# Fused attention and gated-recurrence kernel: VectorE's loop instructions read one SBUF tensor at most, two small products move to GpSimd

## The reference

```
c   = cross_attention(x, cond)                    # 16 heads of 8, one key per head: softmax over 16
q,k,v = heads(c @ Wq), heads(c @ Wk), heads(c @ Wv)   # 16 heads h, 8 dims d
q = softmax(q over d);  k = elu(k) + 1
ctx = cumsum over h of k[d] * v[e];   ctx /= cumsum over h of k[d] + eps
x = x + (sum over d of q[d] * ctx[d, e]) @ Wo + bo
for each of the 128 tokens:                       # a gated recurrence, h0 = cond
    m, o = split(sigmoid([x_t, h] @ w_W + w_b))
    h = o * h + (1 - o) * tanh(x_t @ wx_W + wx_b + m * (h @ wh_W + wh_b))
x = x + experts(hs)                               # 8 experts, relu then square, the top 2 by router logits
```

## Time and profile before

| | |
|---|---|
| median of 3 runs | 627.83 us (627.83 to 629.28) |
| span of the profiled execution, first to last instruction | 625.2 us |
| median less that span (the profiled execution has no other time of its own) | 2.6 us |
| busy: TensorE, VectorE, ScalarE, GpSimd | 480.3, 514.4, 291.4, 208.7 us |
| mean granted TensorE clock | 0.806 of full |

### The profile page before, as it was taken

How to read it: one execution, slowest core, us unless ns; L and a number is a source line. 1 busy time by engine, 2 the same in 40 slices (tenths; PEclk the granted TensorE clock), 3 DMA queues, 4 the chain that set the end, 5 groups by cost and what they waited for, 6 DMA issues and landing times.

```text
span 625.2 us, 10470 instructions
## 1 busy us (share of the span) xinstructions
PE 480.3 (77%) x2559; PEld 362.0 (58%) x2559; DVE 514.4 (82%) x1403; ACT 291.4 (47%) x1084; POOL 208.7 (33%) x192
## 2 busy tenths in 40 slices
PE   6998467877777778877777777778877777777897
PEld 4876145556556556665655556556655655555575
DVE  4777799888988888888888988888888888988852
ACT  4554222444544455444444544455444444544465
POOL 5544433333333332222333333332222333333100
PEclk9999555677888888777777788888777777788899
DMA  5210000000000000000000000000000000000000
GB/s 158 71 35 1 0 0 2 0 5 5 6 4 3 5 4 4 4 4 4 4 4 4 4 2 2 4 4 4 4 4 4 4 4 4 4 3 3 8 6 14
DMA packets 12648, 6.44 MB, mean 10 GB/s; under 512 B 801, under 2 KB 12626, under 8 KB 12626
## 3 DMA queue, kind: packets, MB, share of 16 engines
q1 hardware_dynamic: 12626, 6.19, 3.5%
HBM read 4.09 MB, written 2.10 MB: 10 GB/s over the span
## 4 chain that ended last, share of the span: by engine, by line
PE 43%; DVE 38%; issue 12%; ACT 2%; SPq 2%; DVEq 1%; DMA 1%
PE bank L380 36%; DVE kvs L978 9%; DVE wo L1051 7%; DVE wo L1058 7%; DVE h L1066 6%; PE bank L555 4%; ACT to L768 2%; DVE gw L1023 1%; PE bank L510 1%; DVE mem L1044 1%; SPq L243 1%; DVE kv L941 1%; DMA xin<-in_x_dram 1%; PE bank L434 1%; DVE qn L970 1%
## 5 line engine op out<-in xcount | busy, mean ns | idle before, releaser
L363 POOL TENSOR_TENSOR qc<-kvs,qn 128x512 f32<-128x512 f32 x64 | 97.1, 1518 | 348.0 <-DVE qn L970 325.6
L380 PE MATMUL bank<-h,gwh 128*128 128x32 f32 x512 | 108.4, 297 | 119.1 <-DVE h L1066 118.7
L380 PEld LDWEIGHTS bank<-h,gwh 128*128 128x128 f32 x512 | 93.1, 226 | 154.2 <-DVE h L1066 152.7
L380 PE MATMUL bank<-w,h 128*128 128x512 f32 x128 | 92.2, 812 | 0.0
L766 ACT ACTIVATE th<-bank 128x32 f32<-128x32 f32 x128 | 25.5, 199 | 140.0 <-PE bank L380 139.8
L739 ACT ACTIVATE hid<-bank,gw 128x128 f32<-128x128 f32 x256 | 75.8, 365 | 30.5 <-PE bank L380 30.3
L978 DVE TENSOR_TENSOR_SCAN kvs<-scan_mask,kv 128x256 f32<-128x256 f32 x128 | 86.3, 697 | 0.0
L351 POOL TENSOR_TENSOR kv<-kv,qkv 128x512 f32<-128x512 f32 x64 | 79.4, 1260 | 10.6 <-DVE kv L941 10.6
L1066 DVE TENSOR_TENSOR_SCAN h<-tm,wo 128x64 f32<-128x64 f32 x128 | 60.6, 474 | 15.7 <-ACT tm L774 14.2
L1044 DVE TENSOR_TENSOR_SCAN mem<-th,bank 128x64 f32<-128x64 f32 x128 | 34.0, 266 | 45.2 <-PE bank L380 44.9
L380 PEld LDWEIGHTS bank<-w,hsq 128*128 128x128 f32 x512 | 65.2, 194 | 7.4 <-issue 0.5
(11 more groups left out here) (137 smaller groups left out, 820.0 us busy)
## 6 DMA issues: line engine op xcount, KB each, us to landing
xin<-in_x_dram SPq DMA_DIRECT2D x8, 256.0 KB, 2.8
out_dram<-res SPq DMA_DIRECT2D x32, 64.0 KB
w<-in_L_ffn_w_all_dram SPq DMA_DIRECT2D x2, 512.0 KB
gwx<-in_L_cond_w_W_dram SPq DMA_DIRECT2D x1, 128.0 KB
gwh<-in_L_cond_w_W_dram SPq DMA_DIRECT2D x1, 128.0 KB
mbias<-gpart SPq DMA_DIRECT2D x6, 0.2 KB, 1.7
cwk<-in_L_cond_Wk_dram SPq DMA_DIRECT2D x1, 64.0 KB
cwv<-in_L_cond_Wv_dram SPq DMA_DIRECT2D x1, 64.0 KB
```

Of the source, the lines that this page charges most:

```text
L363: pool.tensor_tensor(qc[:, a:b, :, :], kvs[:, a * D:b * D, :].rearrange("p (d e) h -> p d e h", d=D // 2), qn[:, p, a:b, :].unsqueeze(2).b ...
L380: return pe.matmul(dst, w, rhs, start=start, stop=True, skip_group_check=True)
```

## The change

Every VectorE instruction of the main loop gets at most one of its tensors from SBUF. Bank 1 (`DV`) no longer holds a gate but VectorE's small operands: the scan mask (256 columns), `den`, `wo`, `qmax`, `qsum` and the router's `chosen` logits. Both gates stand in bank 0 (`Z`): their bias comes in by a product with ones for both, and one tanh takes both halves after TensorE's second gate product, so the memory's product comes third, not second. `keys` and `queries` become plain two-tensor instructions on GpSimd (the relu on the keys is now a second eviction on ScalarE). The router replaces the logits that are not chosen instead of taking the chosen ones out, so that `two_largest`, `taken` and a copy fall away. `exp_qk` stands one step earlier in ScalarE's queue. VectorE's queue is in a new order: each step's four instructions stand together as `update`, and `finish` comes before the third update, `taken_inverse` directly behind it.

```diff
--- before.py
+++ after.py
@@ -136,23 +131,25 @@
...
-        th = sb("th", [P, B, 2])
-        to = sb("to", [P, B])
+        gt = sb("gt", [P, 2, B, 2])
...
-        wo = sb("wo", [P, B, 2])
...
-        dl, gex = sb("dl", [P, 2, NE]), sb("gex", [P, 2, NE])
...
+        dl = sb("dl", [P, NE])
...
+        scan_mask = DV[:, 0:D * D * H // 4]
+        den = DV[:, 256:384].rearrange("p (d h) -> p d h", h=H)
+        wo = DV[:, 384:448].rearrange("p (b i) -> p b i", i=2)
+        qmax, qsum, chosen = DV[:, 448:464], DV[:, 464:480], DV[:, 480:488]
...
@@ -342,6 +335,18 @@
             split(pool.tensor_tensor(gres[:, 1, :], gres[:, 0, :], gpart[:, 1, :], ALU.subtract))
             pool.tensor_copy(gpart[:, 2, :], gres[:, 1, :]).then_inc(gsplit, 1)
+            def keys(t, p):
+                pool.wait_ge(ex_done, t + 1)
+                at_least(pool, k_sum, t)
+                pool.tensor_tensor(kv[:, D * D:, :], qkv[:, p, 1, :, :], ex[:, p, 1, :, :], ALU.add)\
+                    .then_inc(k_ready, 1)
+            def queries(t, p):
+                pool.wait_ge(d_rec, 2 * t + 2)
+                pool.tensor_tensor(qn[:, p, :, :], ex[:, p, 0, :, :], rden[:, :, :], ALU.mult).then_inc(qn_done, 1)
             def outer(t, p, half):
                 a, b = half * D // 2, (half + 1) * D // 2
@@ -366,7 +371,11 @@
             def iteration(t, p, has):
                 if has(2):
+                    queries(t + 2, p)
                     weigh(t + 2, p, 0)
+                if has(3):
+                    keys(t + 3, 1 - p)
+                if has(2):
                     weigh(t + 2, p, 1)
                 if has(3):
                     outer(t + 3, 1 - p, 0)
@@ -518,11 +527,11 @@
...
-                at_least(pe, th_done, STEPS * t)
-                mm(ZH[:, 0:TOK], hbias[:, :], ones[:, :])
-                mm(ZH[:, 0:TOK], gwx[:, 0:P], xs, start=False)
-                at_least(pe, to_done, STEPS * t)
-                mm(ZO[:, 0:TOK], gwx[:, P:2 * P], xs)
+                at_least(pe, ga_done, STEPS * t)
+                mm(Z[:, 0:TOK], zbias[:, 0:P], ones[:, :])
+                mm(Z[:, TOK:2 * TOK], zbias[:, P:2 * P], ones[:, :], start=False)
+                mm(Z[:, 0:TOK], gwx[:, 0:P], xs, start=False)
+                mm(Z[:, TOK:2 * TOK], gwx[:, P:2 * P], xs, start=False)
...
@@ -570,10 +579,10 @@
...
-                mm(ZH[:, col:col + B], gwh[:, 0:P], h, start=False).then_inc(zh_ps, 1)
+                mm(Z[:, col:col + B], gwh[:, 0:P], h, start=False)
+                mm(Z[:, TOK + col:TOK + col + B], gwh[:, P:2 * P], h, start=False).then_inc(z_ps, 1)
                 mm(MEM[:, 2 * s * B:2 * (s + 1) * B], whw[:, :], h.unsqueeze(2).broadcast_to([P, B, 2]),
...
-                mm(ZO[:, col:col + B], gwh[:, P:2 * P], h, start=False).then_inc(zo_ps, 1)
...
@@ -707,7 +715,9 @@
...
-                act.activation(qkv[:, p, :, :, :].rearrange("p w d h -> p (w d h)"), QKV[:, P:], ACT.Copy)\
+                act.activation(qkv[:, p, 1, :, :].rearrange("p d h -> p (d h)"), QKV[:, 2 * P:3 * P], ACT.Relu)
+                act.activation(qkv[:, p, 0:3:2, :, :].rearrange("p w d h -> p w (d h)"),
+                               QKV[:, P:].rearrange("p (w n) -> p w n", w=3)[:, 0:3:2, :], ACT.Copy)\
...
@@ -752,21 +762,18 @@
...
-            def gate_exp(t):
+            def gate_exp(t, p):
...
-                at_least(act, gw_done, t)
-                act.activation(gex[:, :, :], dl[:, :, :], ACT.Exp, scale=0.5).then_inc(g_exp, 1)
+                act.activation(gw[:, p, :], dl[:, :], ACT.Exp, scale=0.5).then_inc(gw_done, 1)
...
-                act.wait_ge(zh_ps, n + 1)
-                act.activation(th[:, :, 1], ZH[:, col:col + B], ACT.Tanh, scale=0.5).then_inc(th_done, 1)
-                act.wait_ge(zo_ps, n + 1)
-                act.activation(to[:, :], ZO[:, col:col + B], ACT.Tanh, bias=gcol[:, 0:1], scale=0.5)\
-                    .then_inc(to_done, 1)
+                act.wait_ge(z_ps, n + 1)
+                act.activation(gt[:, :, :, 1], Z[:, 0:2 * TOK].rearrange("p (g n) -> p g n", g=2)[:, :, col:col + B],
+                               ACT.Tanh, scale=0.5).then_inc(ga_done, 1)
...
@@ -796,6 +803,8 @@
...
                     memory_tanh(t, 0)
+                if has(3):
+                    exp_qk(t + 3, q)
...
@@ -805,11 +814,9 @@
                 if has(0):
...
-                    gate_exp(t - 1)
+                    gate_exp(t - 1, q)
                 if has(0):
                     memory_tanh(t, 1)
-                if has(3):
-                    exp_qk(t + 3, q)
...
                 if has(0):
@@ -932,42 +943,31 @@
...
-                                  qmax[:, :].unsqueeze(1).broadcast_to([P, D, H]), ALU.subtract).then_inc(ex_ready, 1)
-            def keys(t, p):
+                                  qmax.unsqueeze(1).broadcast_to([P, D, H]), ALU.subtract).then_inc(ex_ready, 1)
+            def query_sum(t, p):
...
-                at_least(dve, kv_done, 2 * t)
-                dve.scalar_tensor_tensor(out=kv[:, D * D:, :], in0=qkv[:, p, 1, :, :], scalar=0.0,
-                                         in1=ex[:, p, 1, :, :], op0=ALU.max, op1=ALU.add).then_inc(k_ready, 1)
-            def query_sum(t, p):
-                dve.tensor_reduce(qsum[:, :], ex[:, p, 0, :, :].rearrange("p d h -> p h d"), AX.X, ALU.add)\
+                dve.tensor_reduce(qsum, ex[:, p, 0, :, :].rearrange("p d h -> p h d"), AX.X, ALU.add)\
...
-                dve.tensor_tensor_scan(flat(kvs[:, D * D:, :]), flat(scan_mask[:, D * D:, :]), flat(kv[:, D * D:, :]),
+                dve.tensor_tensor_scan(flat(kvs[:, D * D:, :]), scan_mask[:, 0:D * H], flat(kv[:, D * D:, :]),
...
-                dve.scalar_tensor_tensor(out=den[:, :, :], in0=kvs[:, D * D:, :], scalar=EPS,
-                                         in1=qsum[:, :].unsqueeze(1).broadcast_to([P, D, H]), op0=ALU.add,
+                dve.scalar_tensor_tensor(out=den, in0=kvs[:, D * D:, :], scalar=EPS,
+                                         in1=qsum.unsqueeze(1).broadcast_to([P, D, H]), op0=ALU.add,
...
+                at_least(dve, qn_done, t)
...
-            def queries(t, p):
-                dve.wait_ge(d_rec, 2 * t + 2)
-                at_least(dve, qc_done, 2 * (t - 1))
-                dve.tensor_tensor(qn[:, p, :, :], ex[:, p, 0, :, :], rden[:, :, :], ALU.mult).then_inc(qn_done, 1)
...
@@ -1039,16 +1031,14 @@
...
-                dve.wait_ge(th_done, n + 1)
+                dve.wait_ge(ga_done, n + 1)
...
-                dve.tensor_tensor_scan(flat(mem[:, :, :]), flat(th[:, :, :]), MEM[:, 2 * s * B:2 * (s + 1) * B],
+                dve.tensor_tensor_scan(flat(mem[:, :, :]), flat(gt[:, 0, :, :]), MEM[:, 2 * s * B:2 * (s + 1) * B],
...
-                n = STEPS * t + s
-                dve.wait_ge(to_done, n + 1)
-                dve.tensor_scalar(wo[:, :, 0], to[:, :], -0.5, 0.5, ALU.mult, ALU.add).then_inc(w_done, 1)
+                dve.tensor_scalar(wo[:, :, 0], gt[:, 1, :, 1], -0.5, 0.5, ALU.mult, ALU.add).then_inc(w_done, 1)
...
@@ -1063,89 +1053,61 @@
                 n = STEPS * t + s
                 dve.wait_ge(tm_done, n + 1)
                 dve.wait_ge(oh_done, n + 1)
-                dve.tensor_tensor_scan(flat(h2[:, p, s, :, :]), flat(tm[:, :, :]), flat(wo[:, :, :]), 0.0, ALU.mult,
+                dve.tensor_tensor_scan(flat(h2[:, p, s, :, :]), flat(tm[:, :, :]), flat(wo), 0.0, ALU.mult,
                                        ALU.add).then_inc(h_done, 1)
+            def update(t, p, s):
+                memory(t, p, s)
+                renewed(t, s)
+                kept(t, p, s)
+                new_h(t, p, s)
             def iteration(t, p, has):
                 q = 1 - p
-                if has(0):
-                    memory(t, p, 0)
-                    renewed(t, 0)
-                if has(-1):
-                    route(t - 1)
-                if has(0):
-                    kept(t, p, 0)
+                if has(2):
+                    inverses(t + 2, 1)
+                if has(1):
+                    add_dims(t + 1, 1)
                 if has(3):
                     head_max(t + 3, q)
-                if has(0):
-                    new_h(t, p, 0)
+                    less_max(t + 3, q)
+                if has(0):
+                    update(t, p, 0)
                 if has(-1):
-                    two_largest(t - 1)
+                    largest_logits(t - 1)
+                    drop_others(t - 1)
                 if has(2):
                     sum_heads(t + 2, 0)
                 if has(-1):
-                    dve.wait_ge(l_lead, t)
-                    dve.wait_ge(l_copy, t)
+                    less_top(t - 1)
                 if has(2):
                     sum_heads(t + 2, 1)
-                elif has(-1):
-                    dve.tensor_copy(gw2[:, 0:1], lead[:, 0:1])
-                if has(-1):
-                    take_out(t - 1)
-                    less_top(t - 1)
-                if has(0):
```

(49 more changed lines are left out.)

89 lines of the change are left out of this document (38 added, 51 removed).

## The result

The changed kernel takes 603.9 us (median of 4 runs, 598.22 to 607.91), beside 627.83 us before (626.4 to 629.28, 4 runs): a ratio of 0.959, 95% interval 0.954 to 0.964. That is faster, by 24 us, but not by the 71 us of the forecast of 557; it lies at the upper end of the range.

A forecast was written before the change was run, and what follows sets the result against it. VectorE instructions held while GpSimd reads SBUF were taken to bound the kernel. Waits of 14.04 plus 0.3 (PSUM) and 0.4 (clock) made 14.7 us per iteration, saving 63 us, plus 7.5 elsewhere: 557 us, range 531 to 604.

The forecast's parts named there:

- the term of the clock: Main loop: TensorE's clock drops in about a quarter of the iterations, 1.5 us each time, taken as 0.4 us per iteration.
- the clock falls in every iteration: Rival, main loop: TensorE's clock drops every iteration, costing 1.5 us each, 15.8 us per iteration, about 587 us; chance 22%.
- m0-m1: Main loop, from the start of an iteration's first memory scan to its second: 2.69 us, limited by VectorE's work.
- m1-m2: Main loop, second to third memory scan: 1.04 us, then 2.84 through TensorE's products and `finish`, an added wait.
- Holds: Main loop: all four VectorE instructions held while GpSimd reads SBUF are freed, 3.9 us per iteration.
- `renewed` is held all the same: Rival, main loop: `renewed` stays held despite writing to PSUM, 16.6 us per iteration, 609 us; chance 8%.
- The loop of waits: Main loop: distances between memory scans sum to 14.04 us per iteration, with waits added ahead of `finish` and `taken_inverse`.
- PSUM operands: Main loop: some 22 VectorE instructions newly read or write PSUM, taken as 0.3 us per iteration.
- GpSimd: Main loop: `queries` and `keys` move to GpSimd at 0.54 us each, hidden with 6.6 us busy of 14.
- Elsewhere: Outside the steady iterations: prologue 5.5 us off, half of iterations 0 and 1's holds off, last three 2 on; 7.5 off.
- a mean clock that stays at 0.8: Sign in the profile after, on TensorE: it would show the prediction wrong; a clock above 0.85 was expected.
- The rival in which TensorE is the bound at the lower clock throughout: Main loop: TensorE without idle at 19.3 us per iteration, slower, about 685 us; chance 5%.

The follow-up runs named there:

- e1: The changed kernel with three unread products on TensorE, two ahead of the fourth step and one ahead of `x_rows`: 540.54 us.
- e9: The changed kernel with only two unread products on TensorE, ahead of the fourth step: 551.55 us.
- e7: The changed kernel with `taken_inverse` alone put back behind the fourth memory scan, `finish` staying ahead of the third step: 522.76 us.
- e8: As e2, but with the 64-column operand `wo` alone moved back from PSUM to SBUF: 595.39 us.
- e2: The changed kernel with `finish` and `taken_inverse` both put back behind the fourth memory scan: 467.23 us.

## Why the forecast was too low

**The step that failed is the term of the clock**: "I take 0.4, a drop in about a quarter of the iterations". It was 2.7 us per iteration from t = 5 to 27 (17.07 against 14.29 and 0.1 for the loop's turn), and 64.6 us over all 27 iterations (450.35 here, 385.74 in e1), where 0.4 times 27 is 11. The 54 us between are more than the whole miss of 47. Two things in the term were wrong.

- How often. The argument against a fall was that no idle time is as long as the 3.85 us that came before the fall in the old kernel. That took the one idle stretch seen at a fall for the least that brings one, and it misread the stretch: its row has a clock of 0.81, so the fall came inside it, about 2.4 us after its start (2 x 0.19 x 3.85 = 1.5 before its end). After the change 1.58 us and 0.75 us of small products did it in t = 16, and 0.71 and 0.67 us in e9. The fall came in every iteration from t = 4 on, not in a quarter.
- How long. 1.5 us was the price of one passage,'s 6.8 us. But the lower clock lasts into the next iteration: t = 17 runs at 0.69 for 18.07 us, so at 1.2 GHz for 11 of them (2 x 0.31 x 18.07). There m0-m1, where I had VectorE as the limit, takes 4.05 instead of 2.73, and m1-m2, where I had TensorE's products at the higher clock, 5.27 instead of 4.03. Hence the rival "the clock falls in every iteration", right in kind, was too cheap as well: it said 587 us. A short fall alone costs less than the 1.5: 0.7 us in e7.

The Trainium skill ("TensorE: Matmul & The Clock Gate", the section "HAM oscillation — how this bites in real kernels") describes a kernel whose clock falls anew in every tile since it waits in every tile. This trace agrees that a wait that repeats makes the loss repeat, 2.7 us an iteration; here the waits were for VectorE, and shorter than the one in its example.

The other steps, in the order of the prediction:

- *Holds*: right. All four went: three instructions are at 0.18 to 0.29 us, 0.16 to 0.28 assumed, and `taken` fell away with its hold. The rival "`renewed` is held all the same" is out: 0.175 us with its output in PSUM, 1.01 with it in SBUF (e8).
- *The loop of waits*: right. m0-m1 2.69 against 2.72 measured in e1; m1-m2 1.04 + 2.84 = 3.88 against 4.03; m2-m3 4.55 against 4.64; m3-m0 2.92 against 2.90. Both new waits are where they were put. One small sum doesn't follow from the row that it names: 0.46 for the head maximum, where the earlier trace rows has 364 ns, 0.28 by its own rule; from start to start the trace after has 0.46 (353.40 to 353.86).
- *PSUM operands*: right, at most 0.3. The sum of 14.04 became 14.29, which leaves 0.25 for these and all that the sum left out, and no instruction grew by over 0.03 us apart from what it waited for. The 1.4 us an iteration that are estimated from the Trainium skill ("VectorE: DVE Perf Modes", the section on the TRN2 errata) would have made it 15.4, which no run shows.
- *GpSimd*: right. The two small products take 0.46 each (0.54 taken), and it is busy 5.84 us of an iteration.
- *Elsewhere*: the prologue gained 6.5 (scan of t = 0 at 83.33 instead of 89.80; 5.5 taken), iterations 0 and 1 7.1 (4 taken), and the end lost 3.9 (46.44 against 42.56 from the scan of t = 29 on; 2 taken), `finish` waiting 2 us in each of two iterations there. Of the 3.9 the clock has 2.9: in e1 the same stretch is 43.56.
- *The signs*: the forecast named a mean clock that stays at 0.8 as a sign of being wrong. It was 0.75.
- *The rival in which TensorE is the bound at the lower clock throughout*: its sign was wrong, but part of it came true. In iterations such as t = 17 TensorE is busy 15.82 of 18.07 us.

The check by addition: the forecast less the clock's 11 us is 546; with the clock kept up the kernel takes 540.5.

What the prediction did not ask is what the two waits are worth taking. It priced them rightly, 2.84 and 4.55, and still took the order as given. Without them an iteration is 11.69 (e2), and the clock's fall does not come.

## What to carry to other kernels

Where VectorE's small instructions are as long as GpSimd's large ones beside them, count their SBUF tensors: moving the one operand that the recurrence uses in each step into PSUM was worth 128 us here (595 against 467, the clock's share included), the other small operands 8 when they went first. When a wait is put into the loop that TensorE waits for, price it twice: once in the chain, and once for the clock, by all of TensorE's idle time close together and not by the longest of it, over the iteration that follows too. A quick test is an idle product in the gap: if more work makes a kernel faster (63 us here, 53 in the kernel before), the clock is the loss; then take the wait away, which gave 137 us and needs no idle product.
